# One query operand instead of two in a graph-layer kernel: max(q+1, min(exp q, 1)), formed a step ahead on VectorE

## What is computed

```python
def _feature_map(x):
    return jax.nn.elu(x) + 1.0
q = (x @ wq + bq).reshape(b, l, NUM_HEADS, DEPTH)     # 8 heads of 32
q = _feature_map(q); k = _feature_map(k)
kv = einsum('blhd,blhe->bhde', k, v);  k_sum = sum(k, axis=1)
qkv = einsum('blhd,bhde->blhe', q, kv)
normalizer = einsum('blhd,bhd->blh', q, k_sum) + 1e-06
out = (qkv / normalizer[..., None]).reshape(b, l, D_MODEL) @ wo + bo
```

## Time and profile before

| | us |
|---|---|
| median of three runs | 2474.34 |
| the profiled execution, whole | 2474.63 |
| its span, first to last instruction | 2472.7 |
| before the loop (sorting, projections, table) | 494.0 |
| the loop, from the first gather to the last addition | 494.0 to 1554.2 |
| of it: first start of a gather to last start | 494.0 to 1533.7 |
| router and experts | 1554.3 to the end |

### The profile page before, as it was taken

The page is one execution under the profiler, slowest core; times in us unless marked ns, Lnnn a source line. Parts: engine busy times, 40 slices in busy tenths (PEclk is TensorE's granted clock), DMA queues, the critical chain, the costliest instruction groups (busy, mean ns, idle before and its releaser), DMA issues.

```text
span 2472.7 us, 50507 instructions
## 1 busy us (share of the span) xinstructions
PE 2159.0 (87%) x11910; PEld 1729.7 (70%) x11911; DVE 1166.6 (47%) x2173; ACT 1148.6 (46%) x2813; POOL 1382.8 (56%) x1357
## 2 busy tenths in 40 slices
PE   2996897588889999999999887757999999999998
PEld 1664775366766666666666665426999999999997
DVE  8885653156665666656666565463222222222221
ACT  3664114266666666666666665652232323232322
POOL 3420787277777777777777776002454545444443
PEclk9998667799999999999999999957999999999999
DMA  4002000333333333333333337366666666666663
GB/s 147 1 9 43 3 4 3 119 104 104 105 105 105 106 104 105 105 105 105 104 106 104 105 105 101 109 207 195 186 175 187 175 186 178 183 181 180 183 178 79
DMA packets 136249, 289.74 MB, mean 117 GB/s; under 512 B 28580, under 2 KB 77920, under 8 KB 136067
## 3 DMA queue, kind: packets, MB, share of 16 engines
q0 software_dynamic: 67552, 137.24, 23.4%
q1 hardware_dynamic: 68643, 151.89, 19.0%
HBM read 251.51 MB, written 34.37 MB: 116 GB/s over the span
## 4 chain that ended last, share of the span: by engine, by line
PE 50%; POOL 13%; issue 11%; DVE 10%; DVEq 10%; DMA 3%; SPq 1%; ACT 0%; POOLq 0%; ACTq 0%
PE B L1584 15%; PE B L1593 15%; PE B L1480 13%; POOL BIG L507 7%; POOL edge_rows L496 6%; DVE ACC L553 4%; DVEq L884 3%; DVEq L713 2%; DVEq L876 2%; PE B L1553 2%; DMA BIG<-table,W2A 1%; DVE W2A L553 1%; PE B L1453 1%; DVE BIG L553 1%; PE B L1572 1%
## 5 line engine op out<-in xcount | busy, mean ns | idle before, releaser
L507 POOL DMA_INDIRECT BIG<-table,W2A x832 | 787.4, 946 | 297.4 <-issue 225.5
L553 DVE TENSOR_TENSOR ACC<-ACC,B 128x512 f32 x832 | 572.3, 688 | 403.5 <-PE B L1480 294.0
L1157 ACT ACTIVATE BIG<-B,SMALL 128x128 f32<-128x128 f32 (+1 forms) x889 | 251.1, 388 | 532.1 <-PE B L1584 532.0
L1480 PE MATMUL B<-BIG,W2A 128*128 128x256 f32 x1664 | 410.1, 390 | 75.7 <-DVE ACC L553 48.7
L1480 PE MATMUL B<-BIG 128*128 128x256 f32 x1664 | 406.2, 388 | 49.2 <-DMA BIG<-table,W2A 27.0
L1480 PEld LDWEIGHTS B<-BIG,W2A 128*128 128x128 f32 x1664 | 286.3, 189 | 176.3 <-issue 149.0
L1584 PEld LDWEIGHTS B<-BIG,W1A 128*128 128x128 f32 x3360 | 396.7, 194 | 6.7 <-DVE BIG L556 1.4
L1480 PEld LDWEIGHTS B<-BIG 128*128 128x128 f32 x1664 | 293.9, 190 | 153.2 <-issue 114.9
L1584 PE MATMUL B<-BIG,W1A 128*128 128x128 f32 x3360 | 397.4, 277 | 1.0 <-DVE BIG L556 1.0
L1593 PE MATMUL B<-W2A,BIG 128*128 x1680 | 380.1, 379 | 0.7 <-DVE BIG L553 0.7
L527 POOL DMA_INDIRECT out_dram<-BIG,SMALL x105 | 170.7, 1626 | 343.9 <-DVE BIG L556 343.9
(11 more groups left out here) (245 smaller groups left out, 2045.2 us busy)
## 6 DMA issues: line engine op xcount, KB each, us to landing
W1A<-in_w SPq DMA_DIRECT2D x105, 1024.0 KB
BIG<-table,W2A POOLq DMA_INDIRECT x832
W2A<-in_w SPq DMA_DIRECT2D x1, 8192.0 KB, 27.2
token_x<-BIG SPq DMA_DIRECT2D x24, 256.0 KB, 2.1
out_dram<-ACC SPq DMA_DIRECT2D x1, 6144.0 KB
W2A<-in_x SPq DMA_DIRECT2D x1, 3584.0 KB, 13.1
table<-ACC SPq DMA_DIRECT2D x2, 1792.0 KB, 10.2
W2A<-in_x SPq DMA_DIRECT2D x1, 2560.0 KB
```

Of the source, the lines that this page charges most:

```text
L507: pool.indirect_dma_start(G[h][:, u, :], None, table, bass.IndirectOffsetOnAxis(ap=dst_T[:, c:c + 1], axis=0)).then_inc(gath[h][u // 2], 16)
L553: return dve.tensor_tensor(o, a, b, op)
L1157: return nc.scalar.activation(o, i, fn, **kw)
L1480: last = mm(B[u][:, k * D:(k + 1) * D], OH[h % 2][:, u, k * P:(k + 1) * P], G[h][:, u, :], start=True, stop=True)
```

## The change

ACT now forms two things for a tile instead of three: exp q and q + 1 (an Identity with a bias of ones). DVE takes the smaller of exp q and 1, and then the larger of that and q + 1, in one instruction (`features`, 128x256, all operands in SBUF), into `q_feat`. PE multiplies `q_feat` alone by `kv_ext`: two products a step instead of four. All of it is a step ahead: in step i ACT forms the operands of tile i+1 before the one-hots of batches 4i and 4i+1, and DVE combines them between the additions of batch 4i+2 and those of batch 4i+3. A new semaphore `q_known` counts the tiles that DVE has combined. `query_products(i)` waits for it, and so does ACT before it overwrites the operands for the next tile. Since the last tile has no successor, the hardware loops of DVE and ACT now end a step earlier, and step 48 is written out.

```diff
--- before.py
+++ after.py
@@ -230,7 +230,7 @@
         NH = P // DEPTH
         kv_ext = grid(W1A, S1 + 640, KD, P + NH)
         ksum = piece(W1A, S1 + 1152, KD)
-        q_neg, q_exp, q_relu = (piece(W1A, S1 + 1200 + 256 * k, D) for k in range(3))
+        q_exp, q_next, q_feat = (piece(W1A, S1 + 1200 + 256 * k, D) for k in range(3))
         mixed, mixedT = piece(W1A, S1 + 1968, D), grid(W1A, S1 + 2224, KD, P)
         q_den = piece(W1A, S1 + 2480, KD * NH)
 
@@ -315,6 +315,7 @@
         stage_ready, scat = sem("stage_ready"), sem("scat")
         table_ready, table_out = sem("table_ready"), sem("table_out")
         wo_in, kvbd_ready = sem("wo_in"), sem("kvbd_ready")
+        q_known = sem("q_known")
         q_terms, q_ps, q_mixed, q_mixedT_ps, q_mixedT, q_out, q_added = (
             sem("q_terms"), sem("q_ps"), sem("q_mixed"), sem("q_mixedT_ps"), sem("q_mixedT"), sem("q_out"), sem("q_added"))
         raw_in, unpacked, unp_T, unp_out, dst_known = sem("raw_in"), sem("unpacked"), sem("unp_T"), sem("unp_out"), sem("dst_known")
@@ -851,6 +852,11 @@
             dve.sem_inc(kvbd_ready, 1)
 
 
+            def features(t):
+                when(dve, tk_v, q_terms, t + 1)
+                dve.scalar_tensor_tensor(out=q_feat, in0=q_exp, scalar=1.0, in1=q_next, op0=ALU.min, op1=ALU.max
+                                         ).then_inc(q_known, 1)
+
             def divide(t):
                 when(dve, tk_v, q_ps, t + 1)
                 when(dve, tk_v, q_mixedT_ps, t)
@@ -895,6 +901,8 @@
                 if not isinstance(i, int) or i > 0:
                     add_attention(i - 1)
                 add_sums(i * BATCHES + 2)
+                if not isinstance(i, int) or i < NT - 1:
+                    features(i + 1)
                 add_sums(i * BATCHES + 3)
 
             def add_batches(i):
@@ -902,9 +910,11 @@
                     add_sums(i * BATCHES + h)
 
             dve.wait_ge(table_out, 16 * (len(PARTS) + 1))
+            features(0)
             add_step(0)
-            with dve.Fori(1, NT) as i:
+            with dve.Fori(1, NT - 1) as i:
                 add_step(i)
+            add_step(NT - 1)
             add_step(NT)
             add_batches(NT + 1)
             with dve.Fori(NT + 2, STEPS) as i:
@@ -1231,13 +1241,10 @@
                 qt = q_all[:, :, bass.ds(t * P, P)]
                 g3 = lambda a: a.rearrange("p (g n) -> p g n", g=KD)
                 if part == 0:
-                    when(act, tk_a, q_ps, t)
-                    cp(g3(q_neg), qt, ACT.Relu, scale=-1.0)
-                elif part == 1:
-                    cp(g3(q_relu), qt, ACT.Relu)
+                    when(act, tk_a, q_known, t)
+                    cp(g3(q_exp), qt, ACT.Exp)
                 else:
-                    act.drain()
-                    cp(q_exp, q_neg, ACT.Exp, scale=-1.0).then_inc(q_terms, 1)
+                    cp(g3(q_next), qt, ACT.Identity, bias=ones[:, 0:1]).then_inc(q_terms, 1)
 
             def transposed_mix(t):
                 when(act, tk_a, q_mixedT_ps, t + 1)
@@ -1256,14 +1263,17 @@
                 for h in range(BATCHES):
                     if h == 3 and (not isinstance(i, int) or i > 0):
                         transposed_mix(i - 1)
-                    if h < 3 and (not isinstance(i, int) or i < NT):
-                        query_terms(i, h)
+                    if h < 2 and (not isinstance(i, int) or i < NT - 1):
+                        query_terms(i + 1, h)
                     onehots(i * BATCHES + h, h)
 
             act.wait_ge(unp_out, 1)
+            query_terms(0, 0)
+            query_terms(0, 1)
             index_step(0)
-            with act.Fori(1, NT) as i:
+            with act.Fori(1, NT - 1) as i:
                 index_step(i)
+            index_step(NT - 1)
             index_step(NT)
             with act.Fori(NT + 1, STEPS) as i:
                 for h in range(BATCHES):
@@ -1447,11 +1457,9 @@
 
             def query_products(t):
 
-                when(pe, tk_t, q_terms, t + 1)
+                when(pe, tk_t, q_known, t + 1)
                 for g in range(KD):
-                    for k, term in enumerate((q_exp, q_relu)):
-                        last = mm(B[5][:, g * D:g * D + P + NH], term[:, g * P:(g + 1) * P], kv_ext[:, g, :],
-                                  start=k == 0, stop=k == 1)
+                    last = mm(B[5][:, g * D:g * D + P + NH], q_feat[:, g * P:(g + 1) * P], kv_ext[:, g, :], start=True, stop=True)
                 last.then_inc(q_ps, 1)
 
             def transpose_mix(t):
```

## The result

The changed kernel takes 2517.75 us (median of 6 runs, 2515.14 to 2525.26) against 2474.12 us for the kernel before beside it (6 runs): a ratio of 1.0179, 95% interval 1.0165 to 1.0192. It is 43.6 us slower. The forecast was 6 us slower, with a range that ended at 2490: the direction was right, the size was not. The profiled execution took 2525.26 us (span 2523.5), the longest of the six; the other five lie within 2515.14 to 2517.85, so sums over this trace come out some 7.5 us above the median.

A forecast was written before the change was run, and what follows sets the result against it. VectorE was taken to bound the loop at 20.23 us a step. 45 steps x 0.21 = 9.5 us, less 3.5 spare, gave 6.0 late; 2474.63 + 6.0 = 2480.6 us, range 2474 to 2490.

The forecast's parts named there:

- What bounds the loop: Loop: VectorE's own 20.23 us a step bounds it, GpSimd's sixteen gathers need 20.02, and TensorE follows VectorE.
- TensorE's and ScalarE's savings: Loop: TensorE saves 0.53 us a step (26 us), ScalarE 0.40 (20 us); both worth nothing, since these engines wait.
- The cost of `features`: VectorE, between batches 4i+2 and 4i+3: the new instruction adds 0.21 us a step, bounded by 0.1 to 0.36.
- The first rival: VectorE's loop: the new operation costs nothing, hidden in a 0.56 us gap; 2474.6 us, no change; chance 0.14.
- The spare time of the gathers: GpSimd running ahead: 9.0 us spare in step 20, 3.5 left of 9.5 lost, so gather 768 starts 6.0 us late.
- ScalarE's wait and the cover of 0.3 us: Head of each step: late one-hots let VectorE be served at 924.7, needed at 925.0; cover 0.3 us, cost nothing.
- third rival: Batch 4i: ScalarE's wait reaches VectorE, first addition over 5.7 us behind `features`; 0.3 excess costs 13.5 us, 2494; chance 0.11.
- TensorE's longer wait: TensorE before batch 4i: waits 2.4 us more for the one-hots each step, costed at nothing.
- The hold of GpSimd by `features`: Loop gathers: held only at their start, 0.07 us a step, 3.6 us of GpSimd's time, not added to the forecast.
- The second rival: Loop gathers: GpSimd held at nearly every `features`, up to 21 us, 2496; chance 0.06 for more than +10.

The follow-up runs named there:

- exp later: Changed kernel with ScalarE's two query operations one batch later, the exponential ahead of batch 4i+1's one-hots: 2480.1 us, ratio 1.0032 against the kernel before.
- TensorE kept busy with 6: Changed kernel with 6 float32 products, read by nobody, behind batch 4i+3 on TensorE: 2492.0 us, ratio 1.0077 against the kernel before.
- wait alone: Kernel before plus a ScalarE wait for batch 4i-2's last addition and one more Relu, nothing new on VectorE: 2521.5 us, ratio 1.0196.
- one-product kernel: Kernel before with one product of min(exp q, 1) for each half of the query operand, max(q, 0) left out: 2474.5 us, ratio 1.0002.
- operation alone: Kernel before with one more two-input VectorE operation at the change's place, result read by nobody, no one waiting for it: 2477.5 us, ratio 1.0017.
- the kernel with the shorter wait: Kernel before with ScalarE's added wait and Relu, waiting only for batch 4i-2's last addition but one, 1.05 us sooner: 2482.0 us, ratio 1.0036.

## Why the prediction was right about the sign and wrong about the size

The loss of 43.6 us comes apart into three, each kernel taken against the kernel before beside it: 6.7 us for the operation with nobody late (exp later), 18.3 - 6.7 = 11.6 for the late one-hots at full clock (TensorE kept busy with 6), and 43.6 - 18.3 = 25.3 for the fallen clock. By the periods: 0.23, 0.20 and 0.70 us a step, the last from a trace 7.5 us above its median. This is one order of taking the causes away. The wait alone has the whole loss without the operation, and its better steps of about 20.6 us are nearly the changed kernel's 20.65: where batch 4i is late anyway, the operation's own 0.23 hardly shows. The prediction had the first part, had the second as a rival, and had not thought of the third.

**What bounds the loop: right.** VectorE at 20.23 us a step above GpSimd's 20.02, and TensorE following. The one-product kernel gave TensorE 0.45 us a step and changed nothing.

**TensorE's and ScalarE's savings worth nothing: right**, though smaller than put. TensorE saves 1.06 - 0.61 = 0.45 us a step, not 0.53, and alone it is worth nothing. ScalarE's saving was not tried alone; exp later has both savings and shows no gain from them.

**The cost of `features`: right.** It was put at 0.21 us a step, and its price where nobody is late is 20.46 - 20.23 = 0.23. In the trace of the changed kernel it starts 900.92 - 900.32 = 0.60 behind an addition (0.61 forecast) and the next addition 901.80 - 900.32 = 1.48 behind it, where it was 1.26 before. The first rival, that it costs nothing, is out.

**The spare time of the gathers: right as a method.** The working said that some 3.5 us of 9.5 would be hidden, +6.0 us and a last gather at 1539.7. Exp later, where nobody is late, came out at +6.7, with its last gather at 1539.8:

```profile
L508 POOL DMA_INDIRECT BIG<-table,W2A x832: 940/946/1191, 494.6 to 1539.8; - x167
```

So the forecast's sum is near that of another order of ScalarE's work. That it meets the last gather within 0.1 us is partly luck: here an operation costs 0.23, not 0.21, and no batch 4i is late, so 10.8 are spare in step 20 and not 9.0. The same working then gives 45 x 0.23 = 10.4 less 10.8 - 26 x 0.23 = 4.8, some 5.6 us; the gathers take 1539.8 - 494.6 - 1039.7 = 5.5 more, and they also start 0.6 later.

**ScalarE's wait and the cover of 0.3 us: this is the step that failed first.** The prediction followed the right way, `features`, exp, one-hots, TensorE, first addition, and got three of its parts right: exp 0.2 behind the operation (901.61 against 900.92 + 0.48 = 901.40), one-hots 0.4 behind the exp's start (0.32), 2.93 for them (904.85 - 901.93 = 2.92). But it let TensorE start at the moment when the one-hots were ready. It starts 905.50 - 904.85 = 0.65 later. From TensorE's start to the addition it is then 906.83 - 905.50 = 1.33, where the earlier trace rows gave 1.24. Together some 0.7 us, more than the cover of 0.3: the addition stands 906.83 - 900.92 = 5.91 behind the start of `features`, beyond the 5.7 that the prediction had named as the sign of its third rival. That rival was right, and its price near: by its own 45 steps an excess of 0.2 is 9 us, where the kernel with TensorE kept busy shows 11.6. The 0.65 is no wait for another engine. The chain of the changed kernel, in order of time, calls it "issue", time in which the engine waits for nothing that the profile shows:

```profile
904.85 0.64 issue
905.50 1.12 PE B L1488 x4
```

In TensorE's stream (`sum_chunks`) the wait for the one-hots comes first, and behind it stand the waits for the bank and the gather, each with its count. The rows of before held a floor for this: TensorE starts batch 84 at 921.10, 0.39 behind the end of the addition that empties the bank, 920.02 + 0.69, and there only the wait for the gather is left. That alone is more than the cover, which should have been counted as none.

**TensorE's longer wait costed at nothing: the step that failed worst.** "PE waits 2.4 us more" was forecast, and the trace has 2.8 more, 3.2 in place of 0.40. It was weighed only by whether VectorE would be hit. What it did besides was to let the clock fall in 23 of 46 steps, so that a batch takes 5.38 us and not 3.69. By the means of the two kinds a step of the worse kind is 22.02 - 20.68 = 1.34 us longer, and 23 of those are some 31 us of VectorE's time, of which 25.3 show in the end. The row for the loop's last steps that stood ahead of the prediction has a clock of 1.00 with idle times of about 1 us and says nothing of idle times of 3. The trace of before does have a long one, behind the loop, where TensorE idles 9.96 us from 1553.4 on. Its windows:

```profile
1553.40:1556.20 2.80, 0.00 (x0) 0.00 (x0) 2.58 (x7) 0.00 (x0) 0.00 (x0) 1.00 0.00 0
...
1563.40:1566.40 3.00, 3.00 (x11) 1.72 (x12) 2.88 (x11) 2.72 (x7) 0.00 (x0) 0.50 0.53 171
```

The clock is down to 0.50 from 1556.4, some 3 us into the idle time, and stays there for the first 3 us of the work that follows. A batch at half clock behind 3.2 us of idle time was a price to weigh, and the prediction put it at nothing.

**The hold of GpSimd by `features`: there, but small.** The Trainium skill (GPSIMD Engine Reference, Specifications) says that GpSimd shares its SBUF interfaces with VectorE and that VectorE's instructions with two SBUF inputs contend with it. The traces agree for a few gathers: seven in the kernel with the operation alone, which lose 1.5 us together, and six of over 1000 ns in the changed kernel, which lose 0.9. The prediction had put 3.6 us on it, for holds as long as the operation; the held gathers end as if they had begun 0.28 to 0.31 us behind the operation's start, not 0.42. The second rival, 21 us, is out.

Left open: why the slow batches come two by two in the changed kernel and, from the eleventh interval on, one in three or four in the kernel with the shorter wait. No kernel here beats the kernel before, and the runs point to none: the operation adds to VectorE, the engine that bounds the loop, and what it saves is on engines that wait.

## What to carry to other kernels

When a change adds a wait on an engine with time to spare, follow it to the next use of everything queued behind it, and count what each engine's stream still has to do between the wait and the work (0.65 us for TensorE here, of which 0.39 stood in the rows of before); where the cover is thinner than that, count it as gone. When the change lets TensorE wait longer, its idle time has a price even where nobody waits for it in that moment: look at the granted clock behind the longest idle times that the trace has, and where it has none as long, bound the batch behind by a run at half clock. A producer placed one batch earlier or a consumer one batch later (both +0.3% here in place of +1.8%) is worth looking for before the new wait is taken as it stands.

## What the runs showed of the hardware

- TensorE's clock fell from 1.00 to 0.50 behind 22 of 44 idle times of 3.17 to 3.29 us in the changed kernel (and once behind 2.37), behind 22 of 45 of 3.14 to 3.19 with the wait alone, and behind 12 of 41 of 2.09 to 2.14 with the wait one addition sooner; behind 0.63 us, and behind the 1.20 us of the kernel before, in none. The fall can come within the batch that follows (1.00 until 948, 0.50 from 949 to 951, 1.00 again from 952), at its start, or ahead of it (0.50 at 899.20 with the wait alone, where the batch begins at 899.39).
- A float32 product of 128x256 is two records of about 0.22 us at full clock (24 records for 12 products, 5.34 us).
- From the end of VectorE's operation to ScalarE's exp that waits for it were 0.2 us; from the end of a 128x1024 activation to TensorE's first matmul 0.65 us, with two more waits and three counts of TensorE's stream in between.
- A gather that started 0.04 to 0.11 us behind a VectorE operation with two SBUF inputs took 1.13 to 1.19 us in place of 0.95 (operation alone).
- A small VectorE operation between two batches cost 0.16 to 0.23 us a step where it is 0.42 to 0.48 us long: part of it lies beside the sequencer's own work for the next batch.
